# A GRU on one Trainium2 core: the update gate's high weights meet both parts of the state in one product of 128 columns

## The reference

```
def step(h, inp):
    x_t, prop = inp
    comb = jnp.concatenate([x_t, h], axis=-1)
    z = jax.nn.sigmoid(comb @ Wz + bz)
    r = jax.nn.sigmoid(comb @ Wr + br)
    comb2 = jnp.concatenate([x_t, r * h], axis=-1)
    h_cand = jnp.tanh(comb2 @ Wh + bh)
    h_new = (1.0 - z) * h + z * h_cand
    h_next = jnp.where(prop, jnp.tanh(h_new @ Wp + bp), h_new)
    return (h_next, h_new)
```

## Time and profile before

| | |
|---|---|
| median of 3 timed runs | 1056.73 us (1056.33 to 1056.75) |
| the profiled execution | 1056.31 us |
| its span of instructions | 1054.5 us |
| TensorE, matmuls | 1044.9 us busy |
| VectorE | 799.2 us busy |
| ScalarE | 689.4 us busy |
| granted TensorE clock | 0.999 |

### The profile page before, as it was taken

The page is one execution under the profiler, slowest core; times in us unless marked ns, Lnnn a source line. Parts: engine busy times, 40 slices in busy tenths (PEclk is TensorE's granted clock), DMA queues, the critical chain, the costliest instruction groups (busy, mean ns, idle before and its releaser), DMA issues.

```text
span 1054.5 us, 53898 instructions
## 1 busy us (share of the span) xinstructions
PE 1044.9 (99%) x23984; PEld 966.2 (92%) x23984; DVE 799.2 (76%) x2692; ACT 689.4 (65%) x1666; POOL 0.2 (0%) x4
## 2 busy tenths in 40 slices
PE   9999999999999999999999999999999999999997
PEld 3477999999999999999999999999999999999997
DVE  6989988877777777777777777777777776666665
ACT  4766767666666666666666666666675666565664
POOL 0000000000000000000000000000000000000000
PEclk9999999999999999999999999999999999999999
DMA  9312211101111001111001110011110000000001
GB/s 325 110 43 83 77 59 43 44 3 44 43 43 44 23 23 44 43 43 43 21 26 43 44 43 22 24 43 43 43 43 23 24 23 24 23 24 23 24 4 43
DMA packets 38344, 47.63 MB, mean 45 GB/s; under 512 B 2144, under 2 KB 33760, under 8 KB 37728
## 3 DMA queue, kind: packets, MB, share of 16 engines
q1 hardware_dynamic: 38112, 44.19, 12.4%
HBM read 27.40 MB, written 16.78 MB: 42 GB/s over the span
## 4 chain that ended last, share of the span: by engine, by line
PE 94%; DVE 4%; ACT 1%; DMA 1%; issue 1%; SPq 0%; DVEq 0%
PE acc L1122 54%; PE x_acc L1047 34%; PE x_acc L953 5%; PE x_acc L1072 1%; DVE mag L628 1%; DMA x_blk<-x_dram 1%; DVE wrec_lo L692 1%; DVE mag_x L631 0%; DVE win_lo L684 0%; ACT gate L504 0%; DVE x_lo L699 0%; ACT wrec_hi L498 0%; DVE x_lo L706 0%; DVE keep L883 0%; DVE x_blk L909 0%
## 5 line engine op out<-in xcount | busy, mean ns | idle before, releaser
L504 ACT ACTIVATE gate<-acc,unscale 128x128 f32<-128x128 f32 x702 | 239.0, 384 | 268.7 <-PE acc L1122 268.4
L1122 PE MATMUL acc<-h_split,wrec_hi 128*128 128x64 f16 x8192 | 343.8, 193 | 0.0
L1047 PE MATMUL x_acc<-x_hi,win_hi 128*128 128x256 f16 x1092 | 297.7, 273 | 0.0
L1047 PE MATMUL x_acc<-x_hi,win_lo 128*128 128x256 f16 x1092 | 297.6, 273 | 0.0
L1047 PE MATMUL x_acc<-x_lo,win_hi 128*128 128x256 f16 x1092 | 297.6, 273 | 0.0
L1122 PEld LDWEIGHTS acc<-h_split,wrec_hi 128*128 128x128 f16 x8192 | 283.1, 98 | 0.0
L1122 PE MATMUL acc<-q_split,wrec_hi 128*128 128x64 f16 x5088 | 215.5, 193 | 0.0
L1122 PE MATMUL acc<-h_split,wrec_lo 128*128 128x64 f16 x4096 | 203.2, 193 | 1.4 <-DVE h_split L898 1.4
L470 ACT ACTIVATE x_part<-x_acc,bias,part_unscale 128x256 f32<-128x256 f32 x312 | 159.0, 561 | 47.5 <-PE x_acc L1047 47.4
L1122 PEld LDWEIGHTS acc<-q_split,wrec_hi 128*128 128x128 f16 x5088 | 179.2, 98 | 0.0
L524 ACT ACTIVATE acc<-x_part,seed_scale 128x256 f32<-128x256 f32 x384 | 172.7, 477 | 0.1
(11 more groups left out here) (116 smaller groups left out, 1059.8 us busy)
## 6 DMA issues: line engine op xcount, KB each, us to landing
out_dram<-x_blk SPq DMA_DIRECT2D x30, 512.0 KB, 3.2
x_blk<-x_dram SPq DMA_DIRECT2D x24, 512.0 KB, 4.2
x_blk<-x_dram SPq DMA_DIRECT2D x3, 1024.0 KB, 8.8
x_blk<-x_dram SPq DMA_DIRECT2D x4, 256.0 KB, 4.0
x_part<-wz_dram SPq DMA_DIRECT2D x4, 256.0 KB, 7.0
x_part<-wh_dram SPq DMA_DIRECT2D x4, 256.0 KB, 6.6
x_part<-wr_dram SPq DMA_DIRECT2D x1, 1024.0 KB, 11.1
x_part<-wz_dram SPq DMA_DIRECT2D x1, 1024.0 KB, 13.3
```

What stands on the lines that cost most here:

```text
L504: nc.scalar.activation(gate[g][:, half, :], acc[g][:, half, :], func, scale=unscale[:, g:g + 1]).then_inc(gate_ready[g], 1)
L1047: mm = nc.tensor.matmul(in_halves(x_acc[bank][:])[:, j], weights[g][:, slot_w, k, j * P:(j + 1) * P], in_halves(values[m % 2][:, slot_x, : ...
L1122: mm = nc.tensor.matmul(acc[g][:, j, :], weights[g][:, k, j * P:(j + 1) * P], values[:, k, lo, :], start=False, stop=False, skip_group_che ...
```

## The change

From step `PAIRED` = 24 on, Z's high weights are not used once for h's high part and once for its low part. `rec_pair` sends both parts, 128 columns, through each of the 16 weight tiles in one matmul. High goes to the first half of Z's bank, low to its second half: two stretches of 64 columns in one destination. So the low part's products come out in a sum of their own, `acc_bank[Z][:, 1]`.

ScalarE copies that sum to SBUF (into `gate[Z]`), VectorE adds it to `acc[Z]` there, and ScalarE's sigmoid now reads the sum from SBUF. VectorE sets the second half back to zero for the next step. Z's low weights with h's upper two chunks, 8 matmuls, move behind C's first 32, where 4 of Z's matmuls stood, and TensorE waits there for ScalarE's copy.

```
+PAIRED = 3 * BLOCK
...
+                if g == Z and t >= PAIRED:
+                    act.wait_ge(z_low_zero, t - PAIRED + 1)
...
-                squash(Z, ACT.Sigmoid, t, WHOLE)
+                if t < PAIRED:
+                    squash(Z, ACT.Sigmoid, t, WHOLE)
+                else:
+                    act.wait_ge(pairs_done, t - PAIRED + 1)
+                    nc.scalar.copy(gate[Z][:], acc_bank[Z][:, 1]).then_inc(z_low_copied, 1)
+                    act.wait_ge(z_sum_ready, t - PAIRED + 1)
+                    nc.scalar.activation(gate[Z][:], gate[Z][:], ACT.Sigmoid, scale=unscale[:, Z:Z + 1]).then_inc(gate_ready[Z], 1)
...
+                if t >= PAIRED:
+
+                    dve.wait_ge(product_done[Z], t + 1)
+                    dve.wait_ge(z_low_copied, t - PAIRED + 1)
+                    nc.vector.tensor_tensor(gate[Z][:], acc[Z], gate[Z][:], ALU.add).then_inc(z_sum_ready, 1)
+                if PAIRED <= t + 1 < T:
+                    if t < PAIRED:
+                        dve.wait_ge(gate_ready[Z], t + 1)
+                    nc.vector.memset(acc_bank[Z][:, 1], 0.0).then_inc(z_low_zero, 1)
...
+            def rec_pair(k_of):
+
+                for k in k_of:
+                    for j in range(KC):
+                        mm = nc.tensor.matmul(acc_bank[Z][:, :, j, :], wrec_hi[Z][:, k, j * P:(j + 1) * P], h_split[:, k],
+                                              start=False, stop=False, skip_group_check=True)
+                return mm
...
-                rec(Z, wrec_hi, h_split, LOW, 0)
-                rec(Z, wrec_lo, h_split, HIGH, 0)
-                rec(Z, wrec_hi, h_split, HIGH, 0)
-                rec(Z, wrec_hi, h_split, LOW, 1)
-                rec(Z, wrec_hi, h_split, HIGH[:1], 1)
+                if t < PAIRED:
...
+                else:
+                    pe.wait_ge(z_low_zero, t - PAIRED + 1)
+                    rec_pair(LOW)
+                    rec_pair(HIGH).then_inc(pairs_done, 1)
...
-                rec(Z, wrec_hi, h_split, HIGH[1:], 1).then_inc(product_done[Z], 1)
+                if t < PAIRED:
+                    rec(Z, wrec_hi, h_split, HIGH[1:], 1).then_inc(product_done[Z], 1)
+                else:
+                    pe.wait_ge(z_low_copied, t - PAIRED + 1)
+                    rec(Z, wrec_lo, h_split, HIGH, 0).then_inc(product_done[Z], 1)
```

More of the change, by code:

```diff
@@ L311, in gru_kernel @@
         q_hi_ready, q_full_ready, q_lo_ready = sem("q_hi_ready"), sem("q_full_ready"), sem("q_lo_ready")
+        pairs_done, z_low_copied, z_low_zero, z_sum_ready = sem("pairs_done"), sem("z_low_copied"), sem("z_low_zero"), sem("z_sum_ready")
         keep_ready, new_ready = sem("keep_ready"), sem("new_ready")
@@ L1151, in _ @@
                 rec(R, wrec_hi, h_split, HIGH, 1).then_inc(product_done[R], 1)
-                rec(Z, wrec_hi, h_split, LOW, 0)
-                rec(Z, wrec_lo, h_split, HIGH, 0)
-                rec(Z, wrec_hi, h_split, HIGH, 0)
-                rec(Z, wrec_hi, h_split, LOW, 1)
-                rec(Z, wrec_hi, h_split, HIGH[:1], 1)
+                if t < PAIRED:
+                    rec(Z, wrec_hi, h_split, LOW, 0)
+                    rec(Z, wrec_lo, h_split, HIGH, 0)
+                    rec(Z, wrec_hi, h_split, HIGH, 0)
+                    rec(Z, wrec_hi, h_split, LOW, 1)
+                    rec(Z, wrec_hi, h_split, HIGH[:1], 1)
+                else:
+                    pe.wait_ge(z_low_zero, t - PAIRED + 1)
+                    rec_pair(LOW)
+                    rec_pair(HIGH).then_inc(pairs_done, 1)
                 if t == 0:
```

## The result

The changed kernel takes 1073.03 us (median of 5 runs, 1071.23 to 1073.21) against 1056.39. The ratio on record, from all of the runs, is 1.0152 with a 95% interval from 1.014 to 1.0165; the two medians by themselves give 1.0158. The forecast was 1071.9 in a range of 1066 to 1079. The profiled execution of the changed kernel is one of 1073.17 us, its span 1071.4 us, 16.9 us more than before.

What follows compares the result with a forecast made beforehand. TensorE's matmul starts bound the kernel, with the R chain as long as the work above it. 10.2 + 2.2 + 2.8 = 15.2 us on 1056.3 gave 1071.5, for the median 1071.9 us, range 1066 to 1079.

Steps and rivals of the forecast that it cites:

- the main term: 8 instead of 4 matmuls behind C's first 32, + 0.117 us a step, less the earlier C start: + 10.2 us.
- stage 20: Steps 7 of a block: TensorE waits for VectorE's sum behind the later keep, 0.21 us in ten steps: + 2.2 us.
- The R chain: R's last matmul through ScalarE's sigmoid and VectorE's q_split to C's first matmul: 1.07 us, against 0.92 of TensorE work.
- C start: Start of the candidate's first matmul in a step; forecast only 0.02 us earlier than before, 0.01 behind a propagation.
- The slack ahead of C: Room between q allowing C's first matmul and its start before the change: 0.02 us, 0.01 behind a propagation.
- what would show it right: Signs listed beforehand, among them TensorE idle about 0.15 us before q_split's first product in nearly every step from 24.
- The copy free: ScalarE's copy of the low sum takes 0.35 us, ready before TensorE needs it: no cost, 5.6 us at worst.
- The later keep: VectorE's keep, behind add and sigmoid, starts at C + 2.47 instead of C + 1.75: 0.72 us later in slot steps.
- The handover of 0.14 us: Time added from the end of a VectorE item to TensorE's start, taken from q_split's product (0.29 needed 0.43).
- The tail: Steps from 112 on, where thin filler leaves little room for the later keep: + 2.8 us together.
- the seeds keep over 0.5 us of room: The two seeds move as far as keep and still have over 0.5 us of room.
- The rule of 81 ns: Skill's price for a 128-column matmul: C start 0.23 us later, 35 us in sum instead of 10; given little weight.

Runs made afterwards that it cites:

- e3: Changed kernel with each pair run as two matmuls of 64 columns, high part then low part, to the same destinations: 1072.67 us (1.0151).
- e8: Changed kernel with 4 more matmuls of 64 columns between the pairs and C, into a bank part nobody reads: 1072.69 us (1.0152).
- e10: Kernel before, no pair or second sum; from step 24 on 32 update-gate matmuls ahead of C and 8 behind C's 32: 1067.15 us (1.0102).
- e1: Changed kernel with 4 of the 8 matmuls of Z's low weights moved from behind C's first 32 to ahead of the pairs: 1061.74 us (1.0052).
- e11: Kernel before, from step 24 on with all 40 update-gate matmuls ahead of C and none behind: 1055.01 us (0.9988).
- e6: Changed kernel with all 8 matmuls of Z's low weights ahead of the pairs and VectorE's add ahead of the slot's low part: 1051.12 us (0.9951).
- e7: Same order as e6, with each pair run as two matmuls of 64 columns: 1055.25 us (0.9989).

## Why the prediction was right, and where its terms were off

Of the 15.2 us in the forecast's sum 14.9 were measured; the main term came out 0.6 too small and stage 20 0.9 too large, and that these two nearly cancel is luck. The two terms that were not foreseen make 1.8 us together; the measured median lies 1.1 us above the forecast.

**The R chain sets the C start: right.** e3, e8, e10 and e1 each show it from another side: the pairs as two passes, four matmuls more, no pairs at all, and 4 matmuls back ahead of C.

**The main term, 10.2 us: 10.8 measured.** The 0.117 was 0.113. The slack ahead of C was read too large. I had 0.43 us from a row rounded to 0.01; unrounded it is 0.439, and C starts 0.438 behind q_split in the changed kernel as well. So the slack was 0.01 us, not 0.02, and in the steps behind a propagation none at all: there TensorE was already waiting about 0.06 us (e11), where the prediction gave it 0.01 of slack. The prediction took "no wait is shown" for "no wait". It made the same slip in what would show it right: some 15 us of TensorE's idle time ahead of q_split's first product. The matmul rows show 3.5 us there, of which 1.7 were ended by VectorE's q_split; the wait itself is there.

**The copy free: right.** It takes 0.37 us (0.35 worked out) and starts at C + 0.30; Z's low weights follow C's 32 matmuls without a gap (509.52 to 510.45 is 32 by 0.029, and no step up to 126 has more).

**The later keep: right.** Worked out C + 2.47, measured C + 2.50; the add at 0.42 (0.43).

**Stage 20: the place right, the size too large.** VectorE's sum started at C + 4.97 as worked out (4.98), but TensorE followed it 0.80 us later, not 0.89, as the rows of step 63 in the changed kernel show (C start, VectorE's sum, stage 20):

```profile
557.78 0.39 PE L1141 MATMUL acc<-q_split,wrec_lo 128*128 128x64 f16 x8
```

```profile
562.75 0.75 DVE L789 SCALAR_TENSOR_TENSOR x_part<-x_acc,part_unscale,x_part 128x512 f32<-128x512 f32 x1
```

```profile
563.55 0.28 PE L1066 MATMUL x_acc<-x_hi,win_hi 128*128 128x256 f16 x1
```

The handover of 0.14 us was taken from q_split's short instruction and put on a long one, where it was 0.05: 0.12 us a step instead of 0.21.

**The tail: right to 0.1 us.** In every step from 112 to 126 R or PROP starts 0.43 us behind h_split, so TensorE waits for it each time.

**Not foreseen.** Step 110: ScalarE's queue (the seeds, two splits of x, three items out of the filler's banks, the seed of C) had no room left there before, and the seeds that now come 0.6 us later push R's gate back by 0.4. The prediction had said that the seeds keep over 0.5 us of room, which fails in this step. And the clock of step 127, 1.4 us in the profiled run. The first is a queue whose idle time I had not read for that step; the second I did not think of, since the 1.40 us of idle there before had left the clock alone.

**The rule of 81 ns.** By the Trainium skill, TensorE: Matmul & The Clock Gate, section Back-to-back issue gap, a pair would have taken about 81 ns in a stream of loads and matmuls. The pairs of this case start 55.9 ns apart with a weight load each, and e6 against e7 confirms it by the time: at 81 ns e6 would have been the slower of the two. The measurement decides.

## What to carry to other kernels

A tuned order hides a chain of other engines behind just enough work. If an edit makes that work shorter, first ask what the shorter work was covering, and move other work into its place: here the same work gave 1073.0, 1061.7, 1054.0 and 1051.1 us by order alone, on TensorE and, for the last, on VectorE. Measure a cover from start to start, or on the weight loads, never by the idle time of matmuls.

## What the runs showed of the hardware

- A matmul of 128 columns, with weights of its own, into two stretches of 64 with 1 KB between their starts keeps the pace that one contiguous stretch has in the filler, 55.9 ns; two of 64 take 58.4.
- A wait of TensorE up to 0.15 us leaves almost no idle time in the rows of its matmuls: 3.5 us over all of the waits ahead of q_split's matmuls, when the weight loads show 19.5.
- 1.87 us without a matmul ahead of step 127 were followed by some 3 us at half clock in all four traces that have them; 1.40 to 1.48 us were not in any of the seven with them.
- The sigmoid of 256 columns takes 0.51 us from SBUF (104 of them), 0.474 from PSUM (24 in the same trace).
